# A two-layer graph kernel on one core: r is transposed in 32x32 blocks by VectorE, with DRAM putting the blocks in place, and W2 runs one graph later

## The chip, the cores and the metric

The kernel runs on one core of a Trainium2 chip. The core has five engines that work side by side, each through its own list of instructions in order: TensorE (PE, matrix products into PSUM), VectorE (DVE), ScalarE (ACT), GpSimd (POOL), and SyncE (SP), which issues the DMAs here. They wait for each other by semaphores. The metric is the time of one execution on the device, in microseconds (us); lower is better.

## The reference

There are 128 graphs of 128 nodes with 512 features. Each goes through two layers, a graph attention with 8 heads and a hypergraph convolution of two steps, each on a normalised copy of x, and added back to x.

```python
h = jnp.maximum(_layernorm(x), 0.0)
x = x + _L0_gnn_ref(h, adj, W, b, a_self, a_neigh)      # 8 heads of attention over adj, ReLU
h = jnp.maximum(_layernorm(x), 0.0)
x = x + _L1_gnn_ref(h, adj, W1, b1, gamma, beta, W2, b2)

def hypergraph_conv(x, adj, W, b):                       # per graph: H = adj != 0
    xw = x @ W.T
    m = Be[:, :, None] * (H.T @ xw)                      # Be, Dn: reciprocals of column and row sums
    return Dn[:, :, None] * (H @ m) + b

def _L1_gnn_ref(...):
    h = jax.nn.relu(hypergraph_conv(x, adj, W1, b1))     # 512 -> 1024
    h = layer_norm(h, gamma, beta)
    y = hypergraph_conv(h, adj, W2, b2)                  # 1024 -> 512
    return y + x
```

## The kernel before

Everything is in float32. A matrix product with weights is made of three: each operand is split into a high part, rounded to what the array multiplies in one pass, and a low part, the rest; high times high, high times low and low times high are added in PSUM (`high`, `low`, `three`).

The graphs go through a software pipeline written by hand. Turn t works on six graphs at once: it loads graph t+4 and normalises it, makes its features (t+3), its attention scores (t+2), the attention and h (t+1), the first product of layer 1 with W1 and the second with W2 (t), and the last product with G, y (t-1). Every engine's list for a turn is written out in `turn(t)`; `turns` runs it for all t, four turns to one pass of a loop in the middle. Nothing reorders it: the position of a line in `turn` is its position in the engine's queue.

The part of the change is layer 1. TensorE multiplies hg (the gathered h) with W1 into p_w1a and p_w1b (`hidden`, 24 matmuls of 512 columns). VectorE scales each half and adds b1 into r (L625, L645), ScalarE applies ReLU in place (L444, L460). W2 needs r with its 1024 columns on the partitions. So TensorE transposes it, four blocks of 128x128 into p_ta and four into p_tb (L825), ScalarE copies each half to rT_hi (L458, L477) and VectorE forms rT_lo as the difference (L668, L720). Then come 24 matmuls with W2 (L799, L800, L804) into p_w1a. VectorE makes z from them with the deviation rs2 (L760), z is split too, and one turn later three matmuls with G give y (L793 to L795), which VectorE adds to `rest` (x1 + h + b2) and SyncE stores.

Beside it stand the steps of the other graphs that a reader meets below: L576 takes the larger of two exponentials (the leaky ReLU inside a softmax), L640 makes inc = (adj != 0), L696 the row maximum of the scores u, L726 x1, L745 to L746 with GpSimd's L359 and L331 the scale and shift of the second layer norm, L492 h, L915 the gather of h with G, L502 hg_hi, with which the next turn's W1 begins. L467 copies the transposed attention, attT. On SyncE a turn has the load of x and adj for graph t+4, four small stores of en_rows and a broadcast load of u from them, and the store of y.

Of the kernel before, what the change touches and what calls it, by code (L numbers as in the profile page):

```python
# [4 lines left out]
F32 = mybir.dt.float32  # L5
# [44 lines left out]
def turns(eng, turn, total, before={}):  # L50


    loops = (total - AHEAD - 2) // UNROLL
    for t in range(-AHEAD, 1):
        if t in before:
            before[t]()
        turn(Graph(t))
    with eng.Fori(0, loops) as k:
        for u in range(1, UNROLL + 1):
            turn(Graph(u, k))  # L60
    for t in range(1 + loops * UNROLL, total + 1):
        turn(Graph(t))


def gnn_two_layers(nc, x, adj2, W0T, b0, a_self, a_neigh, W1T, b1, gammaT, betaT, W2T, b2, out):
# [13 lines left out]
    with ctx:  # L79
# [40 lines left out]
        rs0, rs1, rs2 = sb("rs0", [P, 1]), sb("rs1", [P, 1]), sb("rs2", [P, 1])  # L120
# [61 lines left out]
        s_stats2, s_mv2, s_ve2, s_rs2, s_rT, s_rT_hi, s_rT_lo = (sem("s_" + n) for n in ("stats2", "mv2", "ve2", "rs2", "rT", "rT_hi", "rT_lo"))  # L182
# [3 lines left out]
        en_rows = nc.dram_tensor("en_rows", [HEADS, N], F32, kind="Internal").ap()  # L186

# [16 lines left out]
        def as_laid(n):  # L204
# [9 lines left out]
                      rest[:, 0, :], rest[:, 1, :]]  # L214
        sums_sb, mean_sb = z, raw[:, 2, 0:D]

        @block.sync
        def _(sp):
# [41 lines left out]
            def turn(t):  # L260
# [24 lines left out]
        def _(pool):  # L285
# [47 lines left out]
            def turn(t):  # L333
# [18 lines left out]
                if g.within(NG):  # L352
                    rstd(g, mv2, ve2, rs2, s_mv2, s_ve2, s_rs2, s_z)
# [17 lines left out]
                if g.within(NG):  # L371

                    s = g.slot(2)
                    if g.has(2):
                        pool.wait_ge(s_y_sb, g.count(2))
                    pool.wait_ge(s_h, g.count())
                    pool.wait_ge(s_x1, g.count())
                    nc.gpsimd.tensor_tensor(rest[:, s, :], x1[:, s, :], h[:, s, :], ALU.add).then_inc(s_xh, 1)
# [3 lines left out]
                    nc.gpsimd.tensor_tensor(rest[:, s, :], rest[:, s, :], b2_bc[:, :], ALU.add).then_inc(s_rest, 1)  # L382
                g = t
# [13 lines left out]
        def _(act):  # L397
# [31 lines left out]
            def turn(t):  # L429
# [43 lines left out]
                g = t  # L473
                if g.within(NG):

                    act.wait_ge(s_rT, g.count(per=2))
                    nc.scalar.activation(rT_hi[:, HALF:DH], p_tb[:, :], ACT.Copy).then_inc(s_rT_hi, 1)  # L477
# [25 lines left out]
                g = t  # L503
# [26 lines left out]
        def _(dve):  # L530
# [47 lines left out]
            def turn(t):  # L578
# [38 lines left out]
                if g.within(NG):  # L617
# [3 lines left out]
                    if g.has(1):  # L621
                        dve.wait_ge(s_rT, g.count(1, per=2))
# [33 lines left out]
                g = t.plus(-1)  # L656
                if g.within(NG):
# [95 lines left out]
                g = t  # L753
                if g.within(NG):
# [5 lines left out]
                    nc.vector.scalar_tensor_tensor(z[:, :], p_w1a[:, :], rs2[:, :], t_bc[:, :],  # L760
# [9 lines left out]
        def _(pe):  # L770
# [57 lines left out]
            def turn(t):  # L828
                g = t
                if g.within(NG):  # L830

                    pe.wait_ge(s_hg_hi, g.count())
                    if g.has(1):
                        pe.wait_ge(s_z, g.count(1))
                    hidden(g, 0, p_w1a)
                    hidden(g, 1, p_w1b)

                    pe.wait_ge(s_r, g.count(per=2) - 1)
                    if g.plus(3).within(NG):
                        pe.wait_ge(s_h0_lo, g.plus(3).count())  # L840
                    transposes(p_ta, r[:, 0:HALF], s_rT)
                g = t.plus(-1)
                if g.within(NG):
# [3 lines left out]
                    if g.plus(2).within(NG):  # L847
                        pe.wait_ge(s_G_sb, g.plus(2).count())
# [34 lines left out]
                g = t  # L883
                if g.within(NG):

                    pe.wait_ge(s_r, g.count(per=2))
                    if g.has(1):
                        pe.wait_ge(s_y_sb, g.count(1))
                    if g.plus(1).within(NG):
                        pe.wait_ge(s_G_sb, g.plus(1).count())  # L890
                    transposes(p_tb, r[:, HALF:DH], s_rT)

                    for m in range(2):
                        if g.base == 0:
                            pe.wait_ge(k_lo2, 1 + m)
                        pe.wait_ge(s_rT_hi, g.count(per=2) - 1 + m)
                        for c in range(m * CB, (m + 1) * CB):
                            high(p_w1a[:, :], rT_hi[:, part(c)], W2_hi[:, c, :], W2_lo[:, c, :], c == 0)
                        pe.wait_ge(s_rT_lo, g.count(per=2) - 1 + m)
                        for c in range(m * CB, (m + 1) * CB):  # L900
                            last = low(p_w1a[:, :], rT_lo[:, part(c)], W2_hi[:, c, :], c == HC - 1)
# [21 lines left out]
                if g.within(NG):  # L923
# [55 lines left out]
```

## Time and profile before

| | |
|---|---|
| median of 3 runs | 2608.23 us (2608.07 to 2610.93) |
| the profiled execution | 2608.28 us, its span 2606.5 us |
| busy: TensorE, VectorE, ScalarE, GpSimd | 2557.4 (98%), 1872.0 (72%), 1503.2 (58%), 1457.5 us (56%) |
| chain of work that ended last, on TensorE | 96% |
| mean granted clock of TensorE | 0.995 of 2.4 GHz |
| share of the 16 DMA engines, GB/s | 17.7%, 61 |

The busy times are of the whole span. In the stretch from 100 to 2560 us the slices of the page are alike: this is the loop, one turn after the other. A row of a timeline has the start in us from the span's start, the duration, the engine, the line, what is written and read, and in brackets how long the engine was idle ahead of it and whose work ended that. Matmuls are pipelined, so the start of the next one tells what a matmul costs, and its duration does not.

### The profile page before, as it was taken

What the parts mean: (1) busy time and instruction counts of PE and PEld (TensorE: products, weight loads), DVE (VectorE), ACT (ScalarE), POOL (GpSimd) and SP (SyncE); (2) the same over time, 40 slices, a digit from 0 to 9 for tenths busy, and PEclk for the clock granted to TensorE, in tenths of its full rate; (3) what the DMA queues carried; (4) which work ended last, traced back from release to release, by engine and by line L of the source; (5) the groups of instructions that cost most, each with busy time, mean ns of one, the idle gap of its engine ahead of it and who ended that gap; (6) DMA issues with size and microseconds to landing.
All of it is one profiled execution on the core that took longest, in us unless ns stands there. A gap on an engine that the chain in (4) does not pass through costs nothing.

```text
span 2606.5 us, 51365 instructions
## 1 busy us (share of the span) xinstructions
PE 2557.4 (98%) x15508; PEld 2245.3 (86%) x15508; DVE 1872.0 (72%) x4638; ACT 1503.2 (58%) x3593; POOL 1457.5 (56%) x2196
## 2 busy tenths in 40 slices
PE   4999999999999999999999999999999999999998
PEld 3788888888888888888888888888888888888886
DVE  6777777767777776777777777777777767777774
ACT  3565555556555555555655555565555555555553
POOL 5555555555555555555555555555555555555553
PEclk8999999999999999999999999999999999999999
DMA  4111111111111111111111111111111111111110
GB/s 152 52 56 66 61 55 63 59 61 61 60 61 55 63 59 61 63 59 61 55 65 58 58 63 59 61 57 64 61 55 63 59 61 62 59 61 55 63 54 25
DMA packets 85593, 158.70 MB, mean 61 GB/s; under 512 B 16832, under 2 KB 33216, under 8 KB 85568
## 3 DMA queue, kind: packets, MB, share of 16 engines
q1 hardware_dynamic: 85568, 158.39, 17.7%
q8 instruction: 12, 0.20, 0.0%
q14 instruction: 13, 0.11, 0.0%
HBM read 124.26 MB, written 34.08 MB: 61 GB/s over the span
## 4 chain that ended last, share of the span: by engine, by line
PE 96%; DVE 0%; issue 0%; POOL 0%; ACT 0%; POOLq 0%; DVEq 0%; ACTq 0%
PE p_w1a L800 14%; PE p_w1a L799 14%; PE p_w1a L804 13%; PE p_att L878 8%; PE p_w1b L800 5%; PE p_w1b L799 5%; PE p_w1b L804 5%; PE p_w1b L915 4%; PE p_att L858 4%; PE p_ta L825 4%; PE p_fa L793 2%; PE p_fa L794 2%; PE p_fa L795 2%; PE p_fb L794 2%; PE p_fb L795 2%; PE p_fb L793 2%
## 5 line engine op out<-in xcount | busy, mean ns | idle before, releaser
L359 POOL TENSOR_TENSOR rs<-ve,halfpow 128x1 f32<-128x1 f32 x128 | 115.3, 901 | 550.3 <-DVE ve L745 550.3
L799 PE MATMUL p_w1a<-W_hi,rT_hi 128*128 128x512 f32 x1024 | 416.4, 407 | 0.0
L800 PE MATMUL p_w1a<-W_lo,rT_hi 128*128 128x512 f32 x1024 | 406.0, 396 | 0.0
L424 ACT ACTIVATE att<-u,shifts 128x128 f32<-128x128 f32 x1024 | 399.7, 390 | 5.0 <-DVE shifts L705 5.0
L425 ACT ACTIVATE att_low<-u,shifts 128x128 f32<-128x128 f32 x1024 | 399.3, 390 | 0.0
L349 POOL TENSOR_TENSOR u<-u,mask 128x1024 f32<-128x1024 f32 x128 | 306.8, 2397 | 37.4 <-DMA u<-en_rows 27.2
L319 POOL TENSOR_TENSOR ve<-mv,eps 128x1 f32<-128x1 f32 x256 | 92.6, 362 | 401.2 <-DVE mv L630 321.9
L804 PE MATMUL p_w1a<-W_hi,rT_lo 128*128 128x512 f32 x1024 | 278.0, 393 | 0.0
L477 ACT ACTIVATE rT_hi<-p_tb 128x512 fp32r<-128x512 f32 x128 | 76.6, 598 | 331.2 <-PE p_tb L825 331.2
L760 DVE SCALAR_TENSOR_TENSOR z<-p_w1a,rs,t_bc 128x512 f32<-128x512 f32 x128 | 96.1, 751 | 218.9 <-PE p_w1a L804 218.9
L878 PE MATMUL p_att<-feats,attT 128*128 128x65 f32 x2048 | 243.2, 272 | 3.5 <-ACT attT L467 3.5
L878 PEld LDWEIGHTS p_att<-feats,attT 128*128 128x128 f32 x2048 | 239.4, 192 | 4.2 <-ACT attT L467 4.2
L804 PEld LDWEIGHTS p_w1a<-W_hi,rT_lo 128*128 128x128 f32 x1024 | 192.9, 188 | 45.0
L800 PEld LDWEIGHTS p_w1a<-W_lo,rT_hi 128*128 128x128 f32 x1024 | 194.2, 190 | 40.1
L799 PEld LDWEIGHTS p_w1a<-W_hi,rT_hi 128*128 128x128 f32 x1024 | 194.0, 189 | 39.5
L765 DVE TENSOR_TENSOR hg_lo<-p_w1b,hg_hi 128x512 fp32r<-128x512 f32 x128 | 88.5, 692 | 190.1 <-ACT hg_hi L502 190.1
L492 ACT ACTIVATE h<-x,nb,rs 128x512 f32<-128x512 f32 x128 | 104.4, 816 | 198.5 <-POOL nb L331 198.5
L799 PE MATMUL p_w1a<-W_hi,hg_hi 128*128 128x512 f32 x512 | 212.2, 414 | 1.1 <-ACT hg_hi L502 1.1
L799 PE MATMUL p_w1b<-W_hi,hg_hi 128*128 128x512 f32 x512 | 203.4, 397 | 0.0
L800 PE MATMUL p_w1b<-W_lo,hg_hi 128*128 128x512 f32 x512 | 203.4, 397 | 0.0
L800 PE MATMUL p_w1a<-W_lo,hg_hi 128*128 128x512 f32 x512 | 202.3, 395 | 0.0
L502 ACT ACTIVATE hg_hi<-p_w1b 128x512 fp32r<-128x512 f32 x128 | 76.7, 600 | 217.6 <-PE p_w1b L915 217.6
(127 smaller groups left out, 7235.6 us busy)
## 6 DMA issues: line engine op xcount, KB each, us to landing
u<-en_rows SPq DMA_DIRECT2D x128, 512.0 KB, 3.5
x_in<-in_x SPq DMA_DIRECT2D x128, 256.0 KB, 2.6
out<-raw SPq DMA_DIRECT2D x128, 256.0 KB, 2.1
adj_in<-in_adj SPq DMA_DIRECT2D x128, 128.0 KB, 2.4
en_rows<-eT SPq DMA_DIRECT2D x512, 1.0 KB
raw<-in_W1T SPq DMA_DIRECT2D x2, 1024.0 KB, 11.0
raw<-in_W2T SPq DMA_DIRECT2D x2, 1024.0 KB, 9.6
raw<-in_W0T SPq DMA_DIRECT2D x1, 1024.0 KB, 5.9
```

The lines of the kernel that those rows point to most:

```text
L349: nc.gpsimd.tensor_tensor(u[:, g.slot(2), :, :], u[:, g.slot(2), :, :], mask[:, :].unsqueeze(1).broadcast_to([P, HEADS, N]), ALU.add).then ...
L359: nc.gpsimd.tensor_tensor(rs1[:, :], ve1[:, :], halfpow[:, :], ALU.pow).then_inc(s_rs1, 1)
L424: nc.scalar.activation(att[:, i, :], u[:, g.slot(2), i, :], ACT.Exp, bias=shifts[:, 0, i:i + 1])
L425: last = nc.scalar.activation(att_low[:, i, :], u[:, g.slot(2), i, :], ACT.Exp, bias=shifts[:, 1, i:i + 1], scale=SLOPE)
L492: nc.scalar.activation(h[:, g.slot(2), :], x1[:, g.slot(2), :], ACT.Relu, bias=nb1[:, :], scale=rs1[:, :]).then_inc(s_h, 1)
L793: mm(dst, hi, w_hi, start=first, stop=False)
L794: mm(dst, hi, w_lo, start=False, stop=False)
L795: return mm(dst, lo, w_hi, start=False, stop=final)
L799: mm(dst, hi, w_hi, start=first, stop=False)
L800: mm(dst, hi, w_lo, start=False, stop=False)
L804: return mm(dst, lo, w_hi, start=False, stop=final)
L878: last = mm(p_o[:, i // HH, i % HH, :], attT[:, i, :], feats[:, g.slot(2), i, :], start=True, stop=True)
```

## The change

- **r's transpose.** When both halves of r have their ReLU, VectorE transposes r (128x1024) in one instruction, each 32x32 block in itself, into rB. SyncE stores rB to a DRAM tensor r_blocks (512 KB), waits for that, and loads it back with four DMAs, one for each group of 32 partitions; the runs of 32 elements (128 B) are picked so that the blocks land where the full transpose has them, in rT. The eight transposes on TensorE are gone.
- **rT_hi and rT_lo** are one instruction of 1024 columns each, from rT in SBUF, for graph t-1: ScalarE's behind the first ReLU of graph t, VectorE's behind the larger-of and ahead of inc.
- **One graph further back.** W2, z and its parts work on graph t-1, y on graph t-2; `turns` runs one turn more. rs2 gets two slots and `rest` four.
- **Places.** rB and rT take what was free of `raw`, `rest` as well; W2's 16 high matmuls now come ahead of all 8 low ones.

```diff
@@ -270,12 +274,21 @@
+                g = t
+                if g.within(NG):
+
+                    sp.wait_ge(s_rB, g.count())
+                    sp.dma_start(r_blocks[:, :], rB).then_inc(s_rB_out, 16)
+                    sp.wait_ge(s_rB_out, g.count(per=16))
+                    for c in range(4):
+                        sp.dma_start(rT[32 * c:32 * (c + 1), :].rearrange("a (k q b) -> a k q b", q=4, b=32),
+                                     r_blocks.rearrange("(q a) (k c b) -> c a k q b", q=4, c=4, b=32)[c]).then_inc(s_rT, 16)
@@ -442,6 +462,13 @@
 
                     act.wait_ge(s_pre, g.count(per=2) - 1)
                     nc.scalar.activation(r[:, 0:HALF], r[:, 0:HALF], ACT.Relu).then_inc(s_r, 1)
+                g = t.plus(-1)
+                if g.within(NG):
+
+                    act.wait_ge(s_rT, g.count(per=64))
+                    if g.has(1):
+                        act.wait_ge(s_w2, g.count(1))
+                    nc.scalar.activation(rT_hi[:, :], rT, ACT.Copy).then_inc(s_rT_hi, 1)
...
-                    act.wait_ge(s_rT, g.count(per=2) - 1)
-                    if g.has(1):
-                        act.wait_ge(s_w2, g.count(1))
-                    nc.scalar.activation(rT_hi[:, 0:HALF], p_ta[:, :], ACT.Copy).then_inc(s_rT_hi, 1)
                     act.wait_ge(s_pre, g.count(per=2))
                     nc.scalar.activation(r[:, HALF:DH], r[:, HALF:DH], ACT.Relu).then_inc(s_r, 1)
...
-                    nc.scalar.activation(rT_hi[:, HALF:DH], p_tb[:, :], ACT.Copy).then_inc(s_rT_hi, 1)
@@ -630,6 +651,11 @@
                     nc.vector.bn_aggr(mv0[:, :], st0[:, :]).then_inc(s_mv0, 1)
                 if t.plus(1).within(NG):
                     larger(t.plus(1), 1)
+                g = t.plus(-1)
+                if g.within(NG):
+
+                    dve.wait_ge(s_rT_hi, g.count())
+                    nc.vector.tensor_tensor(rT_lo[:, :], rT, rT_hi[:, :], ALU.subtract).then_inc(s_rT_lo, 1)
...
                 g = t
                 if g.within(NG):
-                    dve.wait_ge(s_rT_hi, g.count(per=2) - 1)
-                    nc.vector.tensor_tensor(rT_lo[:, 0:HALF], p_ta[:, :], rT_hi[:, 0:HALF],
-                                            ALU.subtract).then_inc(s_rT_lo, 1)
                     dve.wait_ge(s_r, g.count(per=2))
+                    if g.has(1):
+                        dve.wait_ge(s_rB_out, g.count(1, per=16))
+                    nc.vector.transpose(rB, r[:, :]).then_inc(s_rB, 1)
                     nc.vector.bn_stats(st2[:, 1, :], r[:, HALF:DH]).then_inc(s_stats2, 1)
...
-                if t.within(NG):
-                    dve.wait_ge(s_rT_hi, t.count(per=2))
-                    nc.vector.tensor_tensor(rT_lo[:, HALF:DH], p_tb[:, :], rT_hi[:, HALF:DH],
-                                            ALU.subtract).then_inc(s_rT_lo, 1)
...
@@ -830,22 +852,17 @@
                 if g.within(NG):
 
                     pe.wait_ge(s_hg_hi, g.count())
-                    if g.has(1):
-                        pe.wait_ge(s_z, g.count(1))
+                    if g.has(2):
+                        pe.wait_ge(s_z, g.count(2))
                     hidden(g, 0, p_w1a)
                     hidden(g, 1, p_w1b)
-
-                    pe.wait_ge(s_r, g.count(per=2) - 1)
-                    if g.plus(3).within(NG):
-                        pe.wait_ge(s_h0_lo, g.plus(3).count())
-                    transposes(p_ta, r[:, 0:HALF], s_rT)
-                g = t.plus(-1)
+                g = t.plus(-2)
                 if g.within(NG):
...
-                g = t
-                if g.within(NG):
-
...
-                    transposes(p_tb, r[:, HALF:DH], s_rT)
...
+                g = t.plus(-1)
+                if g.within(NG):
+
+                    pe.wait_ge(s_rT_hi, g.count())
+                    for c in range(HC):
+                        if g.base == 0 and c % CB == 0:
+                            pe.wait_ge(k_lo2, 1 + c // CB)
+                        high(p_w1a[:, :], rT_hi[:, part(c)], W2_hi[:, c, :], W2_lo[:, c, :], c == 0)
+                    pe.wait_ge(s_rT_lo, g.count())
+                    for c in range(HC):
+                        last = low(p_w1a[:, :], rT_lo[:, part(c)], W2_hi[:, c, :], c == HC - 1)
                     last.then_inc(s_w2, 1)
```

On VectorE, from the scaling of r's first half to the second set of statistics. Before:

```order
L625 SCALAR_TENSOR_TENSOR r<-p_w1a,inv,b_bc 128x512
L630 BN_AGGR mv<-st 128x2
L574 REGISTER_ALU
L576 TENSOR_TENSOR att<-att,att_low 128x512
L640 TENSOR_SCALAR inc<-adj_in 128x256
L645 SCALAR_TENSOR_TENSOR r<-p_w1b,inv,b_bc 128x512
L651 TENSOR_REDUCE G<-inc 128x1
L655 BN_STATS st<-r 128x6
L662 REGISTER_ALU
L663 SCALAR_TENSOR_TENSOR raw<-p_tb,inv,rest 128x512
L668 TENSOR_TENSOR rT_lo<-p_ta,rT_hi 128x512
L671 BN_STATS st<-r 128x6
```


and with the change:

```order
L651 BN_AGGR mv<-st 128x2
L595 REGISTER_ALU
L597 TENSOR_TENSOR att<-att,att_low 128x512
L658 TENSOR_TENSOR rT_lo<-raw,rT_hi 128x1024
L666 TENSOR_SCALAR inc<-adj_in 128x256
L671 SCALAR_TENSOR_TENSOR r<-p_w1b,inv,b_bc 128x512
L677 TENSOR_REDUCE G<-inc 128x1
L681 BN_STATS st<-r 128x6
L689 SCALAR_TENSOR_TENSOR raw<-p_tb,inv,raw 128x512
L695 REGISTER_ALU
L696 STREAM_TRANSPOSE raw<-r 128x1024
L697 BN_STATS st<-r 128x6
```


rT_lo stands ahead of inc and of the second half of r; the block transpose has the place of the first rT_lo. The second rT_lo, further down behind the attention's scaling, is gone.

On ScalarE, the instructions behind the exponentials. Before:

```order
L444 ACTIVATE r<-r 128x512
L448 REGISTER_ALU
L451 ACTIVATE xn<-x_in,nb,rs 128x512
L457 REGISTER_ALU
L458 ACTIVATE rT_hi<-p_ta 128x512
L460 ACTIVATE r<-r 128x512
L467 ACTIVATE attT<-p_att 128x1024
L477 ACTIVATE rT_hi<-p_tb 128x512
L480 ACTIVATE G_hi<-G 128x128
```


and with the change:

```order
L464 ACTIVATE r<-r 128x512
L468 ISA
L470 REGISTER_ALU
L471 ACTIVATE rT_hi<-raw 128x1024
L475 REGISTER_ALU
L478 ACTIVATE xn<-x_in,nb,rs 128x512
L483 ACTIVATE r<-r 128x512
L490 ACTIVATE attT<-p_att 128x1024
L501 ACTIVATE G_hi<-G 128x128
```


rT_hi stands right behind the ReLU of r's first half, with a wait for DMAs ahead of it, and ahead of xn.

On SyncE, one turn. Before:

```order
L229 ISA
L229 DMA x_in<-in_x 128x512
L230 ISA
L230 DMA adj_in<-in_adj 128x256
L269 DMA en_rows<-eT 8x32 x4
L270 REGISTER_ALU
L271 DMA u<-en_rows 128x1024
L278 ISA
L278 DMA out<-raw 128x512
```


and with the change:

```order
L233 DMA x_in<-in_x 128x512
L234 ISA
L234 DMA adj_in<-in_adj 128x256
L273 DMA en_rows<-eT 8x32 x4
L274 REGISTER_ALU
L275 DMA u<-en_rows 128x1024
L280 REGISTER_ALU
L282 ISA
L282 DMA out<-raw 128x512
L287 DMA r_blocks<-raw 128x1024
L288 REGISTER_ALU
L290 DMA raw<-r_blocks 32x32x32 x4
```


The store of rB and the four loads of rT follow the store of y; the next turn's load of x stands behind them.

## Rows read from the trace of the kernel before

**Rows 1.** The page: busy us (share, instructions); shares of the last chain.

```profile
PE 2557.4 (98%) x15508; PEld 2245.3 (86%) x15508; DVE 1872.0 (72%) x4638; ACT 1503.2 (58%) x3593; POOL 1457.5 (56%) x2196
...
PE 96%; DVE 0%; issue 0%; POOL 0%; ACT 0%; POOLq 0%; DVEq 0%; ACTq 0%
```

**Rows 2.** Timeline, TensorE: start us, us, engine line op out<-in xcount [idle <-releaser].

```profile
1398.44 0.48 PE L799 MATMUL p_w1a<-W_hi,hg_hi 128*128 128x512 f32 x1
...
1404.09 0.60 PE L825 MATMUL p_ta<-ident,r 128*128 128x128 f32 x4
1404.45 0.48 PE L793 MATMUL p_tb<-z_hi,G_hi 128*128 128x512 f32 x1
...
1409.28 0.61 PE L825 MATMUL p_tb<-ident,r 128*128 128x128 f32 x4
1409.64 0.48 PE L799 MATMUL p_w1a<-W_hi,rT_hi 128*128 128x512 f32 x1
...
1416.03 1.05 PE L915 MATMUL p_w1b<-G,h 128*128 128x128 f32 x8
...
1418.23 0.48 PE L799 MATMUL p_w1a<-W_hi,hg_hi 128*128 128x512 f32 x1
```

**Rows 3.** Timeline, VectorE, the same turn.

```profile
1399.07 0.21 DVE L605 STREAM_TRANSPOSE eT<-e_blk 128x32 f32<-128x32 f32 x1
...
1401.60 0.75 DVE L625 SCALAR_TENSOR_TENSOR r<-p_w1a,inv,b_bc 128x512 f32<-128x512 f32 x1 [0.82 <-PE p_w1a L804]
...
1402.36 0.66 DVE L576 TENSOR_TENSOR att<-att,att_low 128x512 f32<-128x512 f32 x1
1402.94 0.28 DVE L640 TENSOR_SCALAR inc<-adj_in 128x256 f32<-128x256 f32 x1
1404.30 0.75 DVE L645 SCALAR_TENSOR_TENSOR r<-p_w1b,inv,b_bc 128x512 f32<-128x512 f32 x1 [1.07 <-PE p_w1b L804]
...
1406.41 0.68 DVE L668 TENSOR_TENSOR rT_lo<-p_ta,rT_hi 128x512 fp32r<-128x512 f32 x1
...
1407.98 1.17 DVE L696 TENSOR_REDUCE neg_max<-u 128x8 f32<-128x1024 f32 x1
```

**Rows 4.** Timeline, ScalarE, the same turn.

```profile
1402.39 0.63 ACT L444 ACTIVATE r<-r 128x512 f32<-128x512 f32 x1 [0.73 <-DVE r L625]
...
1406.31 1.03 ACT L467 ACTIVATE attT<-p_att 128x1024 f32<-128x1024 f32 x1 [0.35 <-PE p_att L858]
...
1414.58 0.82 ACT L492 ACTIVATE h<-x,nb,rs 128x512 f32<-128x512 f32 x1 [1.52 <-POOL nb L331]
```

**Rows 5.** Timeline, GpSimd, the same turn.

```profile
1402.52 0.54 POOL L319 TENSOR_TENSOR ve<-mv,eps 128x1 f32<-128x1 f32 x1 [2.46 <-DVE mv L630]
...
1404.05 0.46 POOL L344 TENSOR_TENSOR mask<-ones,adj_in 128x128 f32<-128x128 f32 x1
```

**Rows 6.** Timeline, VectorE, turn 0: the larger-of beside a GpSimd instruction.

```profile
73.34 2.37 DVE L576 TENSOR_TENSOR att<-att,att_low 128x512 f32<-128x512 f32 x1
```

**Rows 7.** Windows: us, busy us of five engines (x), PEclk, DMA share, GB/s.

```profile
1399.80:1401.60 1.80, 1.80 (x10) 1.44 (x9) 0.99 (x2) 1.80 (x7) 0.27 (x1) 1.00 0.02 2
```

**Rows 8.** The page, DMA issues: out<-in engine op xcount, KB each, us to landing.

```profile
u<-en_rows SPq DMA_DIRECT2D x128, 512.0 KB, 3.5
...
out<-raw SPq DMA_DIRECT2D x128, 256.0 KB, 2.1
```

**Rows 9.** Timeline, TensorE, turn 0.

```profile
79.61 2.61 PE L878 MATMUL p_att<-feats,attT 128*128 128x65 f32 x16 [1.29 <-ACT attT L467]
```

**Rows 10.** Window, turn 0 (columns of rows 7).

```profile
81.00:82.00 1.00, 1.00 (x6) 1.00 (x6) 0.90 (x4) 0.00 (x0) 0.35 (x1) 0.50 0.06 16
```

**Rows 11.** Timeline, TensorE, the last graph: W1's first matmul, transposes, W2's first.

```profile
2585.12 0.50 PE L799 MATMUL p_w1a<-W_hi,hg_hi 128*128 128x512 f32 x1 [0.69 <-ACT hg_hi L502]
...
2593.15 0.63 PE L825 MATMUL p_tb<-ident,r 128*128 128x128 f32 x4 [1.05 <-DVE raw L663]
2593.54 0.48 PE L799 MATMUL p_w1a<-W_hi,rT_hi 128*128 128x512 f32 x1
```

More of the change, by code:

```diff
@@ L50, in turns @@
 def turns(eng, turn, total, before={}):
-    loops = (total - AHEAD - 2) // UNROLL
-    for t in range(-AHEAD, 1):
+    loops = (total - AHEAD - 3) // UNROLL
+    for t in range(-AHEAD, 2):
         if t in before:
@@ L58, in turns @@
     with eng.Fori(0, loops) as k:
-        for u in range(1, UNROLL + 1):
+        for u in range(2, UNROLL + 2):
             turn(Graph(u, k))
-    for t in range(1 + loops * UNROLL, total + 1):
+    for t in range(2 + loops * UNROLL, total + 2):
         turn(Graph(t))
@@ L181, in gnn_two_layers @@
         s_hg, s_hg_hi, s_hg_lo, s_w1, s_pre, s_r = (sem("s_" + n) for n in ("hg", "hg_hi", "hg_lo", "w1", "pre", "r"))
-        s_stats2, s_mv2, s_ve2, s_rs2, s_rT, s_rT_hi, s_rT_lo = (sem("s_" + n) for n in ("stats2", "mv2", "ve2", "rs2", "rT", "rT_hi", "rT_lo"))
+        s_stats2, s_mv2, s_ve2, s_rs2, s_rB, s_rB_out, s_rT, s_rT_hi, s_rT_lo = (sem("s_" + n) for n in ("stats2", "mv2", "ve2", "rs2", "rB", "rB_out", "rT", "rT_hi", "rT_lo"))
         s_w2, s_z, s_z_hi, s_z_lo, s_y, s_y_sb = (sem("s_" + n) for n in ("w2", "z", "z_hi", "z_lo", "y", "y_sb"))
@@ L371, in turn @@
                 if g.within(NG):
-                    s = g.slot(2)
-                    if g.has(2):
-                        pool.wait_ge(s_y_sb, g.count(2))
+                    s, s4 = g.slot(2), g.slot(4)
+                    if g.has(4):
+                        pool.wait_ge(s_y_sb, g.count(4))
                     pool.wait_ge(s_h, g.count())
                     pool.wait_ge(s_x1, g.count())
-                    nc.gpsimd.tensor_tensor(rest[:, s, :], x1[:, s, :], h[:, s, :], ALU.add).then_inc(s_xh, 1)
+                    nc.gpsimd.tensor_tensor(rest[:, s4, :], x1[:, s, :], h[:, s, :], ALU.add).then_inc(s_xh, 1)
                     if g.base == 0:
@@ L621, in turn @@
                     if g.has(1):
-                        dve.wait_ge(s_rT, g.count(1, per=2))
+                        dve.wait_ge(s_rB, g.count(1))
                     if g.plus(4).within(NG):
@@ L752, in turn @@
                     larger(t.plus(2), 0)
-                g = t
+                g = t.plus(-1)
                 if g.within(NG):
@@ L846, in turn @@
                     pe.wait_ge(s_G_lo, g.count())
-                    if g.plus(2).within(NG):
-                        pe.wait_ge(s_G_sb, g.plus(2).count())
+                    if g.plus(3).within(NG):
+                        pe.wait_ge(s_G_sb, g.plus(3).count())
                     three(p_tb[:, :], G_hi[:, :], G_lo[:, :], z_hi[:, :], z_lo[:, :],
@@ L882, in turn @@
                     spread()
-                g = t
+                g = t.plus(-1)
                 if g.within(NG):
[L886 to L890, printed above, removed]
-                    transposes(p_tb, r[:, HALF:DH], s_rT)
[L893 to L901, printed above, removed]
+                    pe.wait_ge(s_rT_hi, g.count())
[6 more added lines that the diff above has]
+                        last = low(p_w1a[:, :], rT_lo[:, part(c)], W2_hi[:, c, :], c == HC - 1)
                     last.then_inc(s_w2, 1)
@@ L930, in turn @@
                         pe.wait_ge(s_G_sb, g.count(1))
+                    if g.has(4):
+                        pe.wait_ge(s_y_sb, g.count(4))
                     mm(p_G, inc[:, g.slot(2), 1, :], beT[:, :], start=True, stop=True).then_inc(s_G, 1)
@@ L935, in turn @@
                     pe.wait_ge(s_xn, g.count())
-                    if t.within(NG):
-                        pe.wait_ge(s_rT_lo, t.count(per=2) - 1)
-                    elif g.has(1):
+                    if g.has(1):
                         pe.wait_ge(s_h0_lo, g.count(1))
```

35 lines of the change are left out of this document (22 added, 13 removed).

## The prediction

> **What bounds the kernel now.** I read the page first: TensorE is busy for 98% of the span and the chain that ended last lies on it for 96% [rows 1]. Then the timeline of one turn of the loop in the middle. On TensorE the turn runs from the first W1 matmul at 1398.44 to the next turn's at 1418.23, 19.79 us, and no row between carries an idle time [rows 2]: each of the other engines waits for TensorE, not the reverse. The question for a change that takes work off TensorE is therefore how far behind it the next chain is. That chain is read from the timelines of VectorE and ScalarE: VectorE waits for the second half of W1's product (L645, 1.07 us idle), works in one go through bn_stats, y, rT_lo, the maximum and x1, GpSimd makes the shift, and ScalarE writes h at 1414.58 to 1415.40 [rows 3, 4]. TensorE takes h at 1416.03 (L915) [rows 2]. Awake at 1415.46 (0.06 for a semaphore), it would have been ready 0.57 us earlier. So 0.57 us is all the slack there is: TensorE's turn can shrink by that much, and a delay of L645 by more than that is a longer turn.
>
> **What TensorE gives up.** Eight transposes of r a turn. Four at 1404.09 hold it until 1404.45, four at 1409.28 until 1409.64 [rows 2]: 0.72 us a turn. By itself that would be a turn of 19.07 us. W2 has the same 24 matmuls, 16 high then 8 low, and takes as long.
>
> **What VectorE gets.** Removed: two rT_lo of 128x512, L668 with 0.68 us and L720 of the same shape; an instruction starts about 0.08 before its forerunner ends (L576 lasts 0.66, L640 starts after 0.58), so 0.60 each in the queue [rows 3]. Added where they stood: one 32x32 transpose of 128x1024. The trace has one of 128x32, 0.21 us, and a reduction of 128x1024, 1.17 us [rows 3]: at one column a cycle the new one is about 1.2 us, 1.12 in the queue. So behind L645 the sum is 1.12 - 0.60 - 0.60, about zero. The other bound is two cycles a column, 2.2 us; no row of 1024 columns is that slow, so I take 1.2.
>
> Added **ahead of L645**: rT_lo of 128x1024, now between the larger-of (L576) and inc (L640). There VectorE idles 1.07 us, which looks like room. But it must wait for rT_hi, and rT_hi now stands on ScalarE behind the first ReLU of the current graph. Walk it: ReLU starts at 1402.39 and lasts 0.63 [rows 4]; rT_hi starts 0.1 before its end, 1402.92. It has 1024 columns: attT has as many and takes 1.03 us [rows 4]; a source in SBUF adds some 0.04. It ends at 1403.99, and rT_lo starts at 1404.03. L576 (512 columns) takes 0.66; 512 more at the rate of the reduction add 0.52: 1.18, 1.10 in the queue. Inc then starts at 1405.13, L645 at 1405.33 instead of 1404.30: **1.03 us late**. Queued behind it on VectorE is all that makes x1 and h; ScalarE's second ReLU and attT move too, so TensorE waits once for attT, and then for h.
>
> **What that makes of a turn.** h ends at 1415.40 + 1.03 = 1416.43, L915 starts at 1416.49 instead of 1416.03. From L915 to the next turn TensorE has the same 2.20 us (1416.03 to 1418.23): next turn at 1418.69. The turn is 20.25 us, 0.46 longer than before, with some 1.2 us of it idle on TensorE. The cycle closes: W1's first half, L625, ReLU, rT_hi, rT_lo, L645, x1, h, L915, the next W1.
>
> **The port.** rT_lo used to read PSUM and SBUF, now two SBUF tiles. In turn 0 the larger-of, which also reads two, took 2.37 us beside a long GpSimd instruction, not 0.66 [rows 6]. At 1404.05, 0.02 us after rT_lo would start, GpSimd starts the mask (L344, 0.46 us) [rows 5]. Whichever comes second waits: rT_lo for up to 0.46, or the mask, in which case inc may wait behind it. Bounds 0 and 0.9 us a turn. I take 0, since rT_lo comes first by these rows and L640 kept its 0.28 us right behind a larger-of that had held GpSimd's L319 for 0.54 [rows 3, 5]; both ends stay for the range. The Trainium skill (SBUF — State Buffer, "Who interferes with whom") says that a VectorE instruction with two SBUF inputs contends with a GpSimd instruction that reads SBUF; by that rule the trace agrees, with the 2.37 us, and without it this paragraph's price would be nothing.
>
> **The DMAs.** A store of 512 KB and four loads that fetch 4096 runs of 128 B, 256 per DMA engine. The transpose ends at about 1408.6. A store of 256 KB lands after 2.1 us and a load of 512 KB after 3.5 [rows 8]; I put the store at 3.0: 1411.7. I put the first packet at 1 us after the issue, half of the 2.1 in which a whole store lands. rT is wanted by rT_hi at 1423.2 in the next turn: 10.5 us for the 256 runs. Tighter is what queues behind them on SyncE: the next turn's x and adj, then en_rows and u. x must have landed for bn_stats, or L625 is late. From the landing of x round to the next: bn_stats 0.60, from L625 to L645 3.73 (1401.60 to 1405.33), to the transpose's end 3.3, store 3.1, first packet 1.0, 256 runs, x and adj 1.9 (three quarters of u's 3.5 less the first us): 13.6 us and the runs. A turn of 20.25 leaves 26 ns a run. Nearest row: in the 1.8 us in which only en_rows is written, 32 runs of 128 B take a 0.02 share of 16 engines, 18 ns each (13 to 22 with the rounding) [rows 7]; four in a turn do not queue, so this may flatter. I take 18: hidden, and en_rows (next issued near 1419.6) finds the rings empty. The Trainium skill (DMA: Bandwidth & Descriptors, "Specifications") gives 512 B as the least transfer at line rate; no row shows long queues of shorter ones.
>
> **Start and end.** Turn 0 has no W2 now and its chain no waits for rT_hi: about -1.5 us. Turns 1 to 124 get 0.46 each: +57. Turn 125 waits for h already: +1. The end: before, the last graph's W2 starts 8.4 us after its W1 (2585.12, 2593.54) [rows 11]. Now it must go through DRAM: transpose done at +9.7, store +12.7, loads (four issues, then 3.5) +17.3, rT_hi +18.4. That is 10 us later, and TensorE, idle for some 6 us, starts at the lower clock: 1.5 more. The sum on the profiled execution: 2608.3 - 1.5 + 57 + 1 + 11.5 = **2676 us**; its own time (span 2606.5, run 2608.28) is the median's, 2608.23, so nothing is to be corrected.
>
> **The rivals.**
> Faster, TensorE stays the bound. It decides at L645: if that is less than 0.57 us late, the turn is shorter than 19.79. With rT_lo wholly inside the idle time h stays at 1415.40, L915 at 1415.46, the turn at 19.22: 125 turns give -71, start and end +10: 2547 us. For it: 1.07 us of idle time just there. Against: rT_hi cannot start before the ReLU. 0.12.
> No change: a shift of 0.5 us, turn 19.72, and the end: within 0.2%. 0.04.
> Slower through the clock. In turn 0 TensorE idled 1.29 us before L878 and the granted clock was at 0.50, 1.2 GHz, shortly after [rows 9, 10]; in the last turn it idled 1.05 and the next matmul of 512 columns took 0.48 as in the loop [rows 11]. Now it idles 1.2 a turn in two pieces. A stretch at 1.2 GHz costs some 1.6 us, of which the wait for h hides half: if half the turns have one, 2676 + 50 to 2676 + 100. 0.14.
> Slower through DRAM. Past 26 ns a run the turn is 13.6 us and the runs: at 35 ns 22.6 us, or 2970 us in all. 0.14. The Trainium skill (VectorE: DVE Perf Modes, "The three transpose paths") says that a plain DMA that transposes by strides is 19 times slower than the crossbar's; by that rule this rival wins, but it is stated for a large innermost stride, and here 32 elements lie together.
> Slower through the transpose: at two cycles a column, 1.05 us more a turn: 2810. 0.06.
> The forecast's own case, with 0 to 0.9 us for the port, 2640 to 2790: 0.50.
>
> **How the numbers follow.** The likeliest is 2676. Slower by over 0.2% (about what a measurement of this kernel can tell): 0.84; within 0.04; faster 0.12. Leaving out the faster case and the worst of DRAM's gives 2600 to 2880.
>
> **What would show it.** Right: turns 20.2 to 20.7 us apart, TensorE idle before L915 for h and before the attention matmuls for attT, VectorE waiting for rT_hi ahead of rT_lo and no longer for W1's second half. Wrong: no idle time on TensorE (the delay was smaller), bn_stats waiting for x_in or rT_hi for a DMA (DRAM), a granted clock under 0.97 in the middle, or a transpose near 2.2 us.

## The result and the profile after

| kernel | median, us | runs | ratio to before |
|---|---|---|---|
| before | 2609.11 | 4 | |
| changed | 2766.68 | 4 | 1.061, interval 1.059 to 1.063 |

The changed kernel is 6% slower. The forecast was 2676 (2600 to 2880): the sign and the range held, the size did not, since the loss is 158 us and not 68. The profiled execution took 2757.67 (span 2755.8), the lowest of the four; the account below is made against it, 149 us over the profiled execution of before.

The page of the changed kernel, busy times and shares of the last chain; rows of before are [rows 1].

```profile
PE 2523.9 (92%) x14484; PEld 2163.4 (79%) x14484; DVE 2068.4 (75%) x4638; ACT 1500.8 (54%) x3465; POOL 1564.4 (57%) x2196
...
DVE 41%; PE 26%; issue 15%; ACT 9%; POOL 5%; DVEq 1%; ACTq 0%; POOLq 0%; DMA 0%; SPq 0%
```

TensorE is down from 98% to 92%, and the last chain runs through VectorE for 41%, not for 0%. Next one turn in the middle (W1's first matmul at 1407.30, the next turn's at 1428.20: 20.90 us, before 19.79 [rows 2]). TensorE's timeline of the changed kernel; L895 are the attention matmuls, L924 is the matmul on h.

```profile
1407.30 0.48 PE L821 MATMUL p_w1a<-W_hi,hg_hi 128*128 128x512 f32 x1
...
1417.11 2.00 PE L895 MATMUL p_att<-feats,attT 128*128 128x65 f32 x16 [0.96 <-ACT attT L490]
...
1425.90 1.16 PE L924 MATMUL p_w1b<-G,h 128*128 128x128 f32 x8 [0.42 <-ACT h L513]
...
1428.20 0.48 PE L821 MATMUL p_w1a<-W_hi,hg_hi 128*128 128x512 f32 x1
```

The two waits forecast are there, for attT and for h. VectorE and GpSimd in the same turn; L646 and L671 are the two halves of r (L625 and L645 before), L658 is rT_lo, L666 inc, L696 the transpose.

```profile
1410.47 0.75 DVE L646 SCALAR_TENSOR_TENSOR r<-p_w1a,inv,b_bc 128x512 f32<-128x512 f32 x1 [0.82 <-PE p_w1a L826]
...
1412.87 1.54 DVE L658 TENSOR_TENSOR rT_lo<-raw,rT_hi 128x1024 fp32r<-128x1024 f32 x1 [0.98 <-ACT rT_hi L471]
1414.33 0.48 DVE L666 TENSOR_SCALAR inc<-adj_in 128x256 f32<-128x256 f32 x1
1414.74 0.74 DVE L671 SCALAR_TENSOR_TENSOR r<-p_w1b,inv,b_bc 128x512 f32<-128x512 f32 x1
...
1416.85 1.23 DVE L696 STREAM_TRANSPOSE raw<-r 128x1024 f32<-128x1024 f32 x1
```

```profile
1412.86 0.47 POOL L357 TENSOR_TENSOR mask<-ones,adj_in 128x128 f32<-128x128 f32 x1
1413.41 1.26 POOL L359 TENSOR_TENSOR mask<-mask,absent 128x128 f32<-128x128 f32 x1
```

rT_lo starts 2.40 us behind the first half of r (forecast 2.43), because it waits for rT_hi, as forecast. But it lasts 1.54, inc 0.48 (0.28 before [rows 3]) and the mask's second instruction 1.26. GpSimd's mask starts at 1412.86, **0.01 us ahead of rT_lo**; the prediction had it 0.02 behind. So the second half of r starts 4.27 us behind the first and not 3.73.

Three of four turns are like this one. In each fourth, the first in the loop's body, GpSimd is a little later and the order is the one forecast, with rT_lo 0.03 us ahead of the mask. Such a turn, two further on:

```profile
1454.75 1.23 DVE L658 TENSOR_TENSOR rT_lo<-raw,rT_hi 128x1024 fp32r<-128x1024 f32 x1 [0.99 <-ACT rT_hi L471]
1455.89 0.55 DVE L666 TENSOR_SCALAR inc<-adj_in 128x256 f32<-128x256 f32 x1
1456.37 0.74 DVE L671 SCALAR_TENSOR_TENSOR r<-p_w1b,inv,b_bc 128x512 f32<-128x512 f32 x1
```

```profile
1454.78 1.51 POOL L357 TENSOR_TENSOR mask<-ones,adj_in 128x128 f32<-128x128 f32 x1
```

Here rT_lo keeps its 1.23 us and the mask waits for it (1.51 instead of 0.46), but inc comes behind the mask and takes 0.55. The second half of r starts 4.02 us behind the first: the forecast order costs too.

### The profile page after: what moved, and what is told of

It reads as the page before. It is cut to its first block, busy times and chain, and to the rows that moved or that the text cites. A ratio compares the mean times of both kernels' runs of the same rounds, so it can differ in the third digit from the quotient of the medians.

```text
span 2755.8 us, 50004 instructions
## 1 busy us (share of the span) xinstructions
PE 2523.9 (92%) x14484; PEld 2163.4 (79%) x14484; DVE 2068.4 (75%) x4638; ACT 1500.8 (54%) x3465; POOL 1564.4 (57%) x2196
## 3 DMA queue, kind: packets, MB, share of 16 engines
q1 hardware_dynamic: 636480, 292.65, 38.5%
## 4 chain that ended last, share of the span: by engine, by line
DVE 41%; PE 26%; issue 15%; ACT 9%; POOL 5%; DVEq 1%; ACTq 0%; POOLq 0%; DMA 0%; SPq 0%
DVE raw L696 5%; PE p_w1b L924 5%; DVE neg_max L722 5%; ACT rT_hi L471 5%; PE p_w1a L821 5%; PE p_w1a L826 5%; PE p_w1a L822 5%; POOL rs L379 4%; ACT h L513 4%; DVE r L646 4%; DVE st L751 3%; DVE raw L740 3%; DVE x L748 3%; DVE st L697 3%; DVE st L681 2%
## 5 line engine op out<-in xcount | busy, mean ns | idle before, releaser
L895 PE MATMUL p_att<-feats,attT 128*128 128x65 f32 x2048 | 255.8, 278 | 117.6 <-ACT attT L490 117.6
L895 PEld LDWEIGHTS p_att<-feats,attT 128*128 128x128 f32 x2048 | 238.2, 191 | 143.4 <-ACT attT L490 143.4
L658 DVE TENSOR_TENSOR rT_lo<-raw,rT_hi 128x1024 fp32r<-128x1024 f32 x128 | 186.2, 1455 | 132.0 <-ACT rT_hi L471 132.0
L826 PE MATMUL p_w1a<-W_hi,rT_lo 128*128 128x512 f32 x1024 | 258.9, 394 | 0.0
L332 POOL TENSOR_TENSOR ve<-mv,eps 128x1 f32<-128x1 f32 x128 | 68.6, 536 | 272.8 <-DVE mv L651 272.8
L924 PE MATMUL p_w1b<-G,h 128*128 128x128 f32 x1024 | 149.5, 290 | 67.2 <-ACT h L513 67.2
L398 POOL TENSOR_TENSOR raw<-x,h 128x512 f32<-128x512 f32 x128 | 163.3, 1276 | 68.0 <-issue 67.2
```

The lines of the kernel that those rows point to most:

```text
L398: nc.gpsimd.tensor_tensor(rest[:, s4, :], x1[:, s, :], h[:, s, :], ALU.add).then_inc(s_xh, 1)
L658: nc.vector.tensor_tensor(rT_lo[:, :], rT, rT_hi[:, :], ALU.subtract).then_inc(s_rT_lo, 1)
L826: return mm(dst, lo, w_hi, start=False, stop=final)
L895: last = mm(p_o[:, i // HH, i % HH, :], attT[:, i, :], feats[:, g.slot(2), i, :], start=True, stop=True)
L924: last = mm(p_w1b[:, c * P:(c + 1) * P], h[:, g.slot(2), c * P:(c + 1) * P], G[:, g.slot(4), 0:N], start=True, stop=True)
```

## The experiments

All of them are edits of one kernel each; "turn" is the distance between W1's first matmuls of two graphs in the middle.

**The mask moved off rT_lo.** GpSimd:

```diff
                     pool.wait_ge(s_in[g.slot(4)], g.uses(4, 32))
                     if g.has(1):
                         pool.wait_ge(s_u, g.count(1))
+                    pool.wait_ge(s_inc, g.count())
```

> The changed kernel, but GpSimd makes the mask of graph t+2 only after VectorE has made inc of graph t+2 (one wait more on GpSimd), so that neither rT_lo nor inc runs beside the mask. Theory (the port): rT_lo 1.54 to 1.23 us, inc 0.48 to 0.28, the mask 1.26 to 0.4, r's second half (line 671) starts 0.54 us earlier after the first, turns 20.9 to 20.36, time about 68 us under the changed kernel's 2767, about 2699 (2690 to 2705), and a little less still if the turns of 21.76 go. Rival (the DRAM round trip or the transpose sets the turn): nothing moves, 2760 to 2770. Rival (the mask is itself on the path, by way of u): later mask, longer turn, over 2770.

Measured 2700.2 us (ratio to before 1.035, with a 95% interval of 1.034 to 1.037), turn 20.37, and 20.67 in every fourth, where the loop starts again. VectorE in the middle:

```profile
1301.04 0.75 DVE L647 SCALAR_TENSOR_TENSOR r<-p_w1a,inv,b_bc 128x512 f32<-128x512 f32 x1 [0.82 <-PE p_w1a L827]
...
1303.44 1.23 DVE L659 TENSOR_TENSOR rT_lo<-raw,rT_hi 128x1024 fp32r<-128x1024 f32 x1 [0.98 <-ACT rT_hi L472]
1304.58 0.29 DVE L667 TENSOR_SCALAR inc<-adj_in 128x256 f32<-128x256 f32 x1
1304.79 0.74 DVE L672 SCALAR_TENSOR_TENSOR r<-p_w1b,inv,b_bc 128x512 f32<-128x512 f32 x1
```

The halves are 3.75 apart and rT_lo takes 1.23. The clash with GpSimd, which the prediction calls the port, was worth 0.53 us in three of four turns (20.90 to 20.37) and 0.26 in each fourth (20.93 to 20.67). That is 57 us between the two profiled executions. The medians are 66 us apart; the other 9 are taken up below, with the clock. With the clash gone the kernel is 24 us above the forecast of 2676. The rivals fall.

**rT_hi early.** ScalarE makes rT_hi before the exponentials of the next graph; TensorE gets a wait that has long been satisfied:

```diff
+                g = t.plus(-1)
+                if g.within(NG):
+                    act.wait_ge(s_rT, g.count(per=64))
+                    if g.has(1):
+                        act.wait_ge(s_w2, g.count(1))
+                    nc.scalar.activation(rT_hi[:, :], rT, ACT.Copy).then_inc(s_rT_hi, 1)
                 if t.plus(1).within(NG):
                     exps(t.plus(1), 1)
...
+                    if t.within(NG):
+                        pe.wait_ge(s_pre, t.count(per=2) - 1)
                     pe.wait_ge(s_rT_hi, g.count())
```

(and the same block is gone from behind r's first ReLU)

> The changed kernel, but ScalarE makes rT_hi of graph t-1 before the second half of the exponentials of graph t+1 and before r's first ReLU, so rT_lo waits only for the larger-of. (W2 on TensorE gets a wait for r's first half, which has long been satisfied, to keep p_w1a ordered in the last turn.) Theory (rT_hi behind the ReLU makes rT_lo and so r's second half late): the exponentials end 0.95 us later, the larger-of starts 0.2 later, rT_lo starts about 0.8 us earlier than now, the turn is 19.8 to 20.1 instead of 20.9, time 2630 to 2665. Rival (DRAM): rT_hi asked for 3 us earlier in the turn waits for a load, turn 20.9 or more. Rival (the delay comes from the port alone): 0.5 us at most.

Measured 2617.8 us (1.004, 1.002 to 1.005), turn 19.70 (20.0 in each fourth): below the range of the theory. GpSimd shows why; L336 and L338 take 0.18 and 0.54 us in the changed kernel.

```profile
1303.01 0.69 POOL L336 TENSOR_TENSOR nm<-mv,neg_one 128x1 f32<-128x1 f32 x1
1303.65 1.54 POOL L338 TENSOR_TENSOR rs<-ve,halfpow 128x1 f32<-128x1 f32 x1
```

rT_lo now starts (1303.56) ahead of L338 and keeps its 1.22 us; this time GpSimd waits, and the mask comes only behind inc. The second half of r is 2.95 us behind the first, 1.32 earlier than in the changed kernel, and the turn is 1.20 shorter. My expectation had left the clash in place. The direction is the theory's; the size comes from rT_hi's place and the port together, and this run does not part them.

**rT_hi and rT_lo early.** As above, and on VectorE rT_lo stands ahead of r's first half:

```diff
                     nc.vector.bn_stats(st0[:, :], x_in[:, g.slot(4), :]).then_inc(s_stats0, 1)
+                g = t.plus(-1)
+                if g.within(NG):
+                    dve.wait_ge(s_rT_hi, g.count())
+                    nc.vector.tensor_tensor(rT_lo[:, :], rT, rT_hi[:, :], ALU.subtract).then_inc(s_rT_lo, 1)
```

> As the kernel with rT_hi early, and VectorE's rT_lo stands ahead of r's first half too (behind bn_stats of x_in), where VectorE idles 0.82 us. Theory (all of the loss of a turn is the delay of r's second half): line 671's instruction starts as soon as W1's second half ends, 1.5 us earlier than now, TensorE waits neither for attT nor for h, turn 19.1 to 19.4, time 2545 to 2590, which is faster than the kernel before. Rival (something else, the transpose or the lag of one graph, costs too): turns 19.8 or more, over 2610. Rival (DRAM): rT_hi waits for a load and turns grow.

Measured 2568.9 us: ratio 0.985 (0.984 to 0.987), 1.5% faster than the kernel before. Turn 19.33. VectorE, second half of r:

```profile
1319.03 0.75 DVE L671 SCALAR_TENSOR_TENSOR r<-p_w1b,inv,b_bc 128x512 f32<-128x512 f32 x1 [0.78 <-PE p_w1b L826]
```

It waits for TensorE again, 5.87 us into the turn (which starts at 1313.16), as before the change (5.86 [rows 2, 3]). So the same VectorE transpose, the same trip through DRAM and the same lag of W2 are in a kernel that gains: what cost 158 us was where rT_hi and rT_lo stand, and the clash with the mask that comes with that place.

**Rows back as rows.** The loads fetch whole rows, so this kernel leaves out putting the blocks in place:

```diff
-                        sp.dma_start(rT[32 * c:32 * (c + 1), :].rearrange("a (k q b) -> a k q b", q=4, b=32),
-                                     r_blocks.rearrange("(q a) (k c b) -> c a k q b", q=4, c=4, b=32)[c]).then_inc(s_rT, 16)
+                        sp.dma_start(rT[32 * c:32 * (c + 1), :], r_blocks[32 * c:32 * (c + 1), :]).then_inc(s_rT, 16)
```

> The changed kernel, but the four loads fetch 32 whole rows of 4 KB each and not 1024 runs of 128 B: the same bytes, issues and waits, but the blocks are not put in place, so the output isn't the reference's. Theory (the loads are hidden: they take 4.7 us per DMA engine of a turn of 20.9): turn unchanged, time within 0.3% of the changed kernel, 2755 to 2775, less 1 to 3 us at the end where rT is waited for; the issue of the four loads is shorter than 3.06 us. Rival (runs of 128 B in DRAM set the turn, or their packets slow x, adj and u): turn shorter by over 0.3 us, under 2730.

Measured 2767.3 us (1.061, 1.059 to 1.063), the changed kernel's time. SyncE, the four issues, in the changed kernel and here:

```profile
1399.82 3.06 SPq L290 DMA_DIRECT2D raw<-r_blocks  x4
```

```profile
1406.33 1.71 SPq L290 DMA_DIRECT2D raw<-r_blocks  x4
```

The runs of 128 B cost SyncE 1.35 us in these rows (in the median an issue takes 0.68 us and not 0.42, so 1.1 us a turn) and the DMA engines some 1.6 us each a turn (their queue's share of the span is 38.5% against 31.2%). They cost the kernel nothing: they are hidden.

**y behind the chain.** On top of both early, VectorE makes y of graph t-2 behind the larger-of of graph t+2, and SyncE stores it last:

```diff
-                    nc.vector.scalar_tensor_tensor(y[:, g.slot(2), :], p_tb[:, :], inv[:, g.slot(4), 0:1],
-                                                   rest[:, g.slot(4), :], ALU.mult, ALU.add).then_inc(s_y_sb, 1)
...
                 if t.plus(2).within(NG):
                     larger(t.plus(2), 0)
...
+                    nc.vector.scalar_tensor_tensor(y[:, g.slot(2), :], p_tb[:, :], inv[:, g.slot(4), 0:1],
+                                                   rest[:, g.slot(4), :], ALU.mult, ALU.add).then_inc(s_y_sb, 1)
```

> As the kernel with rT_hi and rT_lo early, and besides VectorE makes y of graph t-2 (0.65 us in the queue) behind the larger-of of graph t+2, where it idles 0.86 us before z, not ahead of the transpose; SyncE stores y last in its turn. In the kernel with both early h still reaches TensorE about 0.25 us late (line 926 starts 0.06 after h ends) and the pipeline restarts with 0.1. Theory (the chain from r's second half to h sets the turn, instruction for instruction): h comes 0.65 earlier and TensorE is the bound again, turn 18.95 to 19.10 instead of 19.33, time 2525 to 2545. Rival (the turn of 19.33 is TensorE's own): no change, 2565 to 2572. Rival (z is late behind y and with it hg or y's matmuls): turn 19.3 or more.

Measured 2528.05 us: 0.969 (0.967 to 0.971), turn 18.98 (some 19.27 in each fourth). In the kernel with both early TensorE waited for h and took it 0.05 us after its end. With 0.65 us less on the chain it takes h 0.19 us after its end, in three of four turns without a wait: TensorE is the bound again. The rivals fall.

**Delays in the kernel before.** The slack of 0.57 us is tried directly: k bn_stats more (0.60 us each) between the larger-of and inc, k = 2 and 4.

```diff
                     larger(t.plus(1), 1)
+                if t.plus(4).within(NG):
+                    if t.plus(4).has(1):
+                        dve.wait_ge(s_spare, t.plus(4).count(1, per=k))
+                    for i in range(k):
+                        nc.vector.bn_stats(spare[:, i, :], x_in[:, t.plus(4).slot(4), :]).then_inc(s_spare, 1)
```

> The kernel before with two bn_stats of x_in more (0.60 us each in the queue, their results unused) on VectorE between the larger-of and inc, where it idles 1.07 us ahead of r's second half. Theory (0.57 us of slack): r's second half 0.13 late, turn still 19.79, time within 4 us of the kernel before. Rival (VectorE has no slack there): 0.1 to 0.2 us a turn, over 2620.

> As with two, but four: 2.40 us more, r's second half 1.33 late in the kernel before, nothing else changed. Theory (0.57 us of slack, then one for one): turn 19.79 + 1.33 - 0.57 = 20.55, or 20.65 with 0.1 for TensorE's restart after a wait, time 2700 to 2720, TensorE idle before the attention matmuls and before line 915 for h. Rival (a delay of r's second half matters less, what costs is the transpose, the DRAM round trip or the lag of W2): under 2670.

Both missed. Two gave 2591.1 us, ratio 0.993 (0.992 to 0.995), *faster*; four gave 2988.9, 1.144 (1.135 to 1.152). With four, most turns are of two kinds, 20.5 us (44 of 123 in the middle, near the 20.55 to 20.65 of the theory) and 23.9 (64); the other 15 are about 22.6 or 25.5. VectorE and GpSimd in one of each kind, the short first:

```profile
1216.80 0.28 DVE L646 TENSOR_SCALAR inc<-adj_in 128x256 f32<-128x256 f32 x1
...
1216.83 2.50 POOL L350 TENSOR_TENSOR u<-u,mask 128x1024 f32<-128x1024 f32 x1 [0.38 <-DMA u<-en_rows]
```

```profile
1367.29 2.35 DVE L646 TENSOR_SCALAR inc<-adj_in 128x256 f32<-128x256 f32 x1
...
1367.10 2.38 POOL L350 TENSOR_TENSOR u<-u,mask 128x1024 f32<-128x1024 f32 x1 [0.17 <-POOL mask L347]
```

Where inc starts 0.03 us ahead of GpSimd's addition it takes 0.28 us; where it starts 0.19 behind it takes 2.35. TensorE then idles 2.30 us for attT, and its granted clock falls from 1.00 (2.4 GHz) to 0.50 (1.2 GHz) (windows of 1 us in that turn, busy times of five engines, granted clock, DMA share, GB/s):

```profile
1371.92 2.25 PE L884 MATMUL p_att<-feats,attT 128*128 128x65 f32 x16 [2.30 <-ACT attT L468]
```

```profile
1373.30:1374.30 1.00, 1.00 (x8) 1.00 (x8) 1.00 (x2) 0.00 (x0) 0.74 (x2) 0.61 0.17 62
1374.30:1375.30 1.00, 1.00 (x6) 0.90 (x5) 0.86 (x6) 0.24 (x1) 0.00 (x0) 0.50 0.00 0
1375.30:1376.30 1.00, 1.00 (x4) 0.81 (x3) 1.00 (x2) 1.00 (x4) 0.00 (x0) 0.50 0.00 0
1376.30:1377.30 1.00, 1.00 (x5) 0.77 (x4) 0.96 (x3) 1.00 (x5) 0.00 (x0) 0.68 0.00 0
```

Two controls follow. **Four, with the mask behind inc** (the edit of the first experiment):

> The kernel before with four bn_stats more, as before, but GpSimd makes the mask of graph t+2 only after inc of graph t+2. With four, turns were of two kinds: 20.5 us where inc started just ahead of u's addition on GpSimd and took 0.28 us, 23.9 where it started 0.2 us behind it and took 2.35, and the granted clock fell to 0.50 after the longer wait. Theory (slack 0.57 and then one for one, the rest is the port): inc always 0.28 us, all turns 20.5, clock 0.99, time 2695 to 2715. Rival (u comes too late for the maximum now): turns 20.6 to 21.0, to 2760. Rival (the long turns come from TensorE's waits alone): still some of 23.9, over 2800.

Measured 2739.3 us (1.050, 1.048 to 1.051), every turn 20.79, clock 0.993. That is above the 2715 allowed, and within the range of the rival that has u come too late for the maximum. The rows tell the two apart: u ends at 1316.21, a small instruction beside it (cnt) stretches from 0.15 to 0.45 us, and the maximum (L703) starts 0.25 us after u's end, without a wait. So it is the port again.

```profile
1312.48 0.75 DVE L652 SCALAR_TENSOR_TENSOR r<-p_w1b,inv,b_bc 128x512 f32<-128x512 f32 x1
...
1315.79 0.45 DVE L691 TENSOR_SCALAR cnt<-G 128x2 f32<-128x2 f32 x1
...
1316.46 1.17 DVE L703 TENSOR_REDUCE neg_max<-u 128x8 f32<-128x1024 f32 x1
```

```profile
1313.84 2.37 POOL L351 TENSOR_TENSOR u<-u,mask 128x1024 f32<-128x1024 f32 x1 [0.16 <-POOL mask L348]
```

r's second half is 3.90 us behind the first (2.70 before), 1.20 late. With the 0.30 of cnt, less the slack of 0.57, and with 0.10 for TensorE's restart after a wait (see below), the turn should be 1.03 longer; it is 1.00 longer. The slack of 0.57 agrees with that.

**The tile alone.** The kernels with more bn_stats had a small tile behind st0. Here it is put into the kernel before, and into the fastest, without an instruction:

```diff
         st0 = sb("st0", [P, 6])
+        spare = sb("spare", [P, 12])
```

> The kernel before with one unused tile of 48 bytes a partition behind st0 in SBUF, which moves every tile behind it by 48 bytes; no instruction is added. The kernel with two bn_stats more had such a tile, and was 18 us faster than the kernel before, with 12 matmuls of 512 columns in 2.74 us and not 2.79. Theory (the place of the stationary tiles in SBUF does that): 12 matmuls in 2.74 us, turn 19.66, time 2588 to 2594. Rival (the two instructions or the later r did it): 2606 to 2612.

> The fastest kernel so far (rT_hi, rT_lo early, y late, 2528 us) with the same unused 48 bytes behind st0. Theory (place in SBUF, TensorE the bound there): turn 18.98 - 0.13 = 18.85, time 2508 to 2515. Rival (no effect of place, or chain of VectorE the bound): 2524 to 2532.

Measured 2591.8 us (0.994, 0.992 to 0.995), turn 19.67, as with two bn_stats; so these two cost nothing, as the slack says, and the whole 18 us goes with the tile. TensorE's matmul with the high part of rT, in the kernel before and with the tile (total us, mean ns):

```profile
L799 PE MATMUL p_w1a<-W_hi,rT_hi 128*128 128x512 f32 x1024 | 416.4, 407 | 0.0
```

```profile
L800 PE MATMUL p_w1a<-W_hi,rT_hi 128*128 128x512 f32 x1024 | 412.3, 403 | 0.0
```

In the fastest kernel it gave 2522.96 us (0.967, 0.966 to 0.968), turn 18.93: 5 us, not 15, and between the ranges of theory and rival. The matmul on h does come 0.13 us earlier in the turn there. But it now starts 0.08 us behind the end of h (0.19 without the tile), and from it to the next W1 TensorE needs 2.29 us and not 2.20, as it does in the other kernels where h has only just come. So 0.05 us of the 0.13 is left. This is the fastest kernel of the study, 3.3% under the kernel before.

## Why the prediction was right and wrong

**Right: bound, slack, path.** The turn's path was named beforehand (W1's first half, ReLU, rT_hi, rT_lo, r's second half, x1, h) with its slack. rT_lo starts 2.40 behind r's first half (2.43 said). The transpose takes 1.23 us (1.2 said) and cancels the two rT_lo: from r's second half to x1 it is 6.85 us, 6.86 before. The trip through DRAM is hidden; rT_hi waits for a load once, in the last turn.

**Wrong: "The port ... I take 0".** This is the step that failed. The prediction had bounds of 0 and 0.9 us and took the lower end, because by its rows rT_lo would start 0.02 us ahead of the mask. It failed twice. First, that margin was smaller than the error of each sum before it: in three of four turns rT_lo came 0.01 behind. From then on it is a handing over: rT_lo is held by the mask's first instruction (1.46 us from its start to inc's, not 1.10), the mask's second by rT_lo, inc by that (0.41 to r's second half, not 0.20). Together 0.57 us on the path, of which the experiment gave back 0.53 a turn. Second, rT_lo's coming first does not make the price 0: in each fourth turn it did come first, the mask waited, inc waited for the mask, and the turn lost 0.26. The prediction named this case ("inc may wait behind it") and set it aside because L640 had kept its 0.28 us behind a held GpSimd instruction. That instruction (L319) is 128x1 and the mask is 128x128, so the row could not stand for it; that the size is the reason is not tested. In all the port cost 57 us. Half the range in place of its lower end would have given about 2730. The Trainium skill (SBUF — State Buffer, "Who interferes with whom") calls the shared pair of ports an exclusive lock: whichever instruction starts first keeps it and the other waits. The trace agrees, in both orders: inc 2.35 us behind an addition of 2.38, GpSimd's L338 1.54 instead of 0.54 behind rT_lo. Where starts lie within hundredths of a us the runs show less than the rule says (last section).

**Smaller sizes.** From the matmul on h to the next W1 TensorE needed 2.20 us before; after a wait it needs 2.30 (1425.90 to 1428.20): 0.10 a turn, 12 us, which the sum left out. Turn 0 starts 0.37 us earlier and is 0.57 us shorter, 0.9 in all and not 1.5. The end cost 13.3 us and not 11.5: W2 of the last graph starts 18.95 us behind its W1 (18.4 said), and its first fourteen matmuls run at the lower clock, 0.44 us each instead of 0.23, 2.9 us where 1.5 was put. For three of four turns: 0.46 forecast + 0.53 port + 0.10 restart = 1.09, measured 1.11. For each fourth: 0.46 + 0.26 + 0.10, and 0.30 that such a turn is longer even without the clash, make 1.12; measured 1.14. The 0.30, 9 us in all, was in no term either.

**The clock.** The rival "slower through the clock" was half there. Two turns of the profiled execution last 21.76 us; this is one (windows, TensorE after its wait for attT, 0.96 us as in the turn shown above):

```profile
2067.00:2068.00 1.00, 1.00 (x4) 0.81 (x4) 1.00 (x1) 0.00 (x0) 0.74 (x2) 0.50 0.98 401
2068.00:2069.00 1.00, 1.00 (x4) 0.80 (x3) 0.86 (x6) 0.11 (x1) 0.00 (x0) 0.50 0.18 70
```

Each costs 0.86 us. The other three executions have lower mean clocks (0.979 to 0.990 against 0.992) and are 7 to 22 us longer; some ten such turns would make up the 9 us from the profiled execution to the median. That is an estimate, and no trace of those executions shows the turns. The trace of the kernel with whole rows, whose turns are otherwise the same, has a mean clock of 0.984 and 13 turns of 21.7 to 21.8 us. In the profiled executions without the clash (mask behind inc, or rT_hi early) no turn of the middle is that long.

**Against the faster rival.** It said 2547 us for a kernel whose r is on time, with a turn of 19.22. The kernel with both early is that kernel: 2568.9, turn 19.33, since TensorE still waits a little and loses the 0.1 of the restart, and 19.53 in each fourth turn.

## What to carry to other kernels

A margin of hundredths of a microsecond between two engines that share a port decides nothing in advance: price both orders, follow each through to the instruction behind (here they cost 0.53 and 0.26 us, neither 0), or take the shared wait off the path. Ask what the chain next to the bound has queued on it, and move whatever waits for another engine (rT_lo) or is not on the chain (y) to where its engine idles; here that turned a loss of 6% into a gain of 3%. A probe that adds a buffer changes addresses too, so time the buffer alone.

## What the runs showed that I had not expected

- A VectorE instruction with one input from SBUF (inc, tensor_scalar of 128x256) is held as well: 2.35 us instead of 0.28. The Trainium skill (SBUF — State Buffer, "Who interferes with whom") gives this rule for two inputs and for VectorE's two-port modes, which it says a tensor_scalar can enter. No row names inc's mode; its 256 columns take 0.28 us, where a reduction of 128 columns (L651) takes 0.27.
- The changeover need not lie at the recorded start. In the kernel with four bn_stats more, inc started 0.005 to 0.066 us *behind* the addition in 14 turns and kept its 0.28 us in each, while the addition grew to 2.5 or 2.6; from 0.074 us on inc was held. rT_lo was held already 0.01 us behind the mask.
- 48 bytes more in SBUF made the 512-column matmuls with split operands start closer (12 in 2.74 us, not 2.79, 1.8%; W2's 24 in 5.35, not 5.43) at the same granted clock of 1.00; 96 bytes (four bn_stats, 5.44 with the mask behind inc) did not. Which tile's place does it is open.
- Runs of 128 B from DRAM cost little: 4096 of them and the store beside them take 4.7 us of each DMA engine a turn (38.5% of 2755.8 us against 17.7% of 2606.5 us before). A run takes 13 ns of an engine; the prediction had put 18. SyncE's price is 0.68 us an issue in the median, where the store of rB takes 0.33.
- Where h sets the turn, each fourth turn, at the start of the loop's body, is 0.2 to 0.3 us longer (19.53 against 19.33, 20.67 against 20.37). I did not follow it up. In the changed kernel it shows as only 0.03, because the port costs less in that turn.
